# Macaron block on one core: when the rows of the folded matrices are loaded, and where the first thought ends

## The chip, the cores and the metric

The kernel runs on one core of a Trainium2 chip. The time is the device time of one launch in microseconds (us). The median of three runs before the change is 2015.07 us (2013.3 to 2016.36). Less is better.

## The reference, cut to what matters

The input x has 2 batches of 2048 tokens with 1024 features, in float32. Three layers follow each other:

```
x = x + 0.5 * ffn(layernorm(x))
x = x + attention(layernorm(x))
x = x + 0.5 * ffn(layernorm(x))

ffn(x):   x_norm  = layer_norm(x, in_gamma, in_beta)
          thought = x_norm[:, -1, :] @ agg_w + agg_b          # the last token of each batch alone
          4 times:  t = layer_norm(thought, pn_gamma, pn_beta)
                    t = gelu(t @ d1_w + d1_b)                 # 1024 -> 4096
                    thought = thought + (t @ d2_w + d2_b)     # 4096 -> 1024
          broadcast = thought @ bc_w + bc_b
          gate = sigmoid(x @ gate_w + gate_b)
          return layer_norm(x + gate * broadcast, out_gamma, out_beta)

attention(x): windows of 128 tokens, each looks at itself and the window before;
          sim = q k^T, squared relu of the kept part, times v, times w_o
```

The gate is a 1024 x 1024 product for all 4096 tokens; the thought is a chain of vector by matrix products for two tokens only, which has to be finished before any token of the batch can leave its ffn.

## The kernel before, in words

The 4096 tokens are 32 tiles of 128. One list, PLAN, made by `whole_plan` (line 556), holds all the pieces of the work in one order, and each of the five engines walks through that same list and does its own part of each piece. So an engine that waits in one piece does nothing of any later piece. SyncE (SP) issues every DMA, in the order of the list, and waits for semaphores in that order too.

Stage 0 and 1 go like this. First PE multiplies wq and wk into one folded matrix, qk ("fold", in float32, L1145 and its like), and stores it row by row in qk_scratch. Then come the gate products of the first 12 tiles (`EARLY`), then the fold of wv and wo into vo (L1149), stored in vo_scratch, and then the gates of the other 20 tiles. A tile's gate is made of two transposes ("turn", L1123, four 128 x 128 blocks each) and six pieces of eight matmuls (L1114). For a tile n+2 VectorE takes the moments ("norm", L1545), GpSimd makes 1/sigma (L2015, L2022), and ScalarE normalises ("norm_h", L1403), and only then can PE turn the tile. ScalarE rounds what was turned (L1341), and VectorE keeps the rest (L1562). The gate comes out of PSUM by VectorE (L1570) and ScalarE's sigmoid (L1416), and is stored (L968). x is loaded by L964.

Both folded matrices must be rounded into a high and a low float16 half before stage 2. For each of the 8 rows of 128 x 1024 this is: load it from the scratch into one of the `ROW_RING` = 3 row slots (`fold_rows`, L956), round it on ScalarE (`round`, L1378), and take the rest on VectorE (`split`, L1658, which ends the use of the row slot). `rounded_ahead` (line 540) writes their order: round k+1, split k, then the k-th of the loads that it is given. These pieces form the list `splits`. The function `paced(main, other, pace)` mixes a list into another: behind each PE piece of the main list it puts `pace` pieces of the other on average, and what is left over stands at the end. `splits` is mixed with 0.56 into the gates of the tiles from `EARLY` to the last `LATE` ones. A "rest" is an empty piece.

The first thought's products run in between. `with_thought` spreads its beats evenly over the whole of stage 0 and 1 but for the last `LATE` tiles, by the pieces' costs, so that the last beat comes about 5 us of such costs before the end. A beat of weights is two units of 128 x 1024 for each of two pairs (L1313 for halves in float16, L1303 for whole float32); the units are loaded by L897 into 10 slots, and a load waits for the beat that used the slot before.

Then come "publish" (L1005, the broadcast row goes to all partitions as thought_row) and the last `LATE` tiles' gates. Into these the preparation of the first group of stage 2 is mixed: two tiles u, each with prep_norm (ScalarE, L1428), prep_beta (L1706), prep_h (L1699, the first to read thought_row), prep_y (L1712), prep_x1 (L1721, L1726), prep_stats, prep_h1 (ScalarE, L1436, L1439), prep_low (VectorE, L1736) and group_turn (SP, L1035, a DMA transpose). What they read is loaded by prep_fetch (L1018 and L1022), which for the first group waits until all rows of vo are split. Besides, `gate_save` (L973) copies the gate's weights away in 8 pieces.

Stage 2 starts with two value products of the first token tile (v, 128 x 512), then the queries (q, 128 x 256), scores, and the collecting of the weighed values (L1248). The preparation of each next group is mixed into it with 1.3 pieces for each PE piece. Stage 3 is the second ffn's gates.

Of the kernel before, what the change touches and what calls it, by code (L numbers as in the profile page):

```python
# [17 lines left out]
KD, KH = D // P, H // P  # L18
NT = T // P
TILES = B * NT  # L20
# [26 lines left out]
X_RING, PAIR_RING, GATE_RING, FOLD_RING, ROW_RING = 3, 2, 2, 2, 3  # L47
# [3 lines left out]

FOLD_SIZES = [2] + [1] * (KD - 2)
FOLD_FROM = [sum(FOLD_SIZES[:j]) for j in range(len(FOLD_SIZES))]
EARLY, LATE = 12, 4
SLACK = 2


# [266 lines left out]
def paced(main, other, pace, counted=None):  # L324

    other, made, due = list(other), [], 0.0
    for piece in main:
        made.append(piece)
        if counted is None or piece[0] in counted:
            due += pace  # L330
            while due >= 1.0:
                due -= 1.0
                if other:
                    made.append(other.pop(0))
    return made + other
# [201 lines left out]
PE_PIECES = {"fold", "turn", "gate", "wo_turn", "q", "v", "score", "collect"}  # L537


def rounded_ahead(m, fetches):  # L540

    out = [("round", m, 0)]
    for k in range(KD):
        out += ([("round", m, k + 1)] if k + 1 < KD else []) + [("split", m, k)] + fetches[k:k + 1]
    return out
# [10 lines left out]
def whole_plan():  # L556
    gate_rows = [("gate_rows",), ("x", 0)] + [("rest",)] * 8
    gate_rows += [("gate_max", k) for k in range(KD)]
    gate_rows += [("scale_t", "gate"), ("rest",), ("scale_a", "gate"), ("rest",), ("scale_b", "gate")]
    gate_rows += rounded_ahead("gate", [])  # L560
    wo_ahead = 3
    gate_rows += [("x", 1), ("x", 2)] + [("wo_rows", n) for n in range(wo_ahead)] + [("norm", 0), ("rest",)]
    gate_rows += [("norm_h", 0), ("norm", 1), ("rest",), ("norm_h", 1), ("turn", 0, 0), ("turn", 0, 1)]
    fold_qk = paced(plan_fold("qk"), gate_rows, 1.0, PE_PIECES)
    fold_qk.append(("fold_store", "qk", KD - 1))
    wo = []
    for n in range(KD):
        wo += [("wv_piece", n), ("wo_turn", n, 0), ("wo_turn", n, 1)]
        if n + wo_ahead < KD:
            wo.append(("wo_rows", n + wo_ahead))  # L570
        if n >= 3:
            wo.append(("top", "wv", n - 3))
    wv_splits, wo_splits = (split_side(m) for m in ("wv", "wo"))
    sides = [("top", "wv", e) for e in range(KD - 3, KD)] + [("scale_t", "wv")] + [("top", "wo", e) for e in range(2)]
    sides += [("scale_a", "wv")] + [("top", "wo", e) for e in range(2, 4)] + [("scale_b", "wv")]
    sides += [("top", "wo", e) for e in range(4, KD)] + [("scale_t", "wo")] + wv_splits[:4]
    sides += [("scale_a", "wo")] + wv_splits[4:6] + [("scale_b", "wo")] + wv_splits[6:] + wo_splits
    early = paced([p for n in range(5) for p in plan_gate(n)], wo, 0.85, PE_PIECES)
    early += paced([p for n in range(5, EARLY) for p in plan_gate(n)], sides, 0.9, PE_PIECES)
    fold_vo = plan_fold("vo") + [("fold_store", "vo", KD - 1)]  # L580
    splits = []
    for m in ("qk", "vo"):
        splits += [("fold_rows", m, 0), ("fold_rows", m, 1), ("scale_t", m), ("rest",), ("scale_a", m), ("rest",), ("scale_b", m)]
        splits += rounded_ahead(m, [("fold_rows", m, k) for k in range(2, KD)])
    splits[8:8] = [("params",)] + [("rest",)] * 5 + [("half_params",)]
    splits[3:3] = [("scale_t", "norm"), ("rest",), ("rest",), ("scale_a", "norm"), ("rest",), ("rest",), ("scale_b", "norm")]
    splits += [("prep_fetch", 0), ("rest",), ("rest",), ("prep_norm", 0), ("prep_beta", 0)]
    gates = paced([p for n in range(EARLY, TILES - LATE) for p in plan_gate(n)], splits, 0.56, PE_PIECES)
    out = [("start",)]
    out += with_thought(fold_qk + early + fold_vo + gates, THOUGHTS.beats[0])  # L590
    out.append(("publish", 0))
    before = [(kind, u) for kind in ("prep_norm", "prep_beta") for u in range(GROUP)]
    prep = [("rest",)] * 2 + [("prep_norm", 1), ("prep_beta", 1)] + [("rest",)] * 4
    prep += [p for p in plan_prep(0) if p not in before]
    late = []
    for n in range(LATE):
        late += plan_gate(TILES - LATE + n) + [("gate_save", k) for k in range(2 * n, 2 * n + 2)]
    out += paced(late, prep, 1.15, PE_PIECES)
    out += [("sigmoid", TILES - 1, 1), ("gate_store", TILES - 1)]
    out.append(("score_scale",))  # L600
    out += plan_stage_2(0, B)
    queries, others = plan_last_group()
    out += with_thought(plan_stage_2(B, GROUPS - 1) + queries, THOUGHTS.beats[1]) + others
    out += plan_stage_3()
    return out


PLAN = whole_plan()


# [1474 lines left out]
```

## Time and profile before

| | us |
|---|---|
| median of the three runs | 2015.07 |
| the profiled execution | 2012.83 |
| its span | 2011.6 |
| PE busy | 1945.9 (97%) |
| VectorE busy | 1300.5 (65%) |
| ScalarE busy | 661.9 (33%) |
| GpSimd busy | 166.4 (8%) |
| DMA engines, mean bytes moved | 276 GB/s |

The span is the time from the first to the last instruction; the profiled execution has 1.2 us around it. A busy engine is one with an instruction in work; PE's matmuls overlap, so their listed lengths are a little longer than their spacing. Stage 1 with its folds lasts until 732 us, stage 2 until about 1669 us, and stage 3 to the end.

### The profile page before, as it was taken

Reading aid. Unit: us, or ns where it says so; the run is one execution under the profiler, and the core shown is the slowest. Engines: PE = TensorE matmul, PEld = TensorE weight load, DVE = VectorE, ACT = ScalarE, POOL = GpSimd, SP = SyncE. Lnnn points to the kernel's source line nnn. Section 1 sums busy time; section 2 is a strip of 40 time slices with the busy share of each in tenths; the row PEclk is TensorE's granted clock in tenths of the full one; section 3 lists DMA queues with packets and bytes.
Section 4 is the critical chain, followed back from the end, with each engine's and each line's share of the span. In section 5 each row is a group of like instructions: output and inputs, shape, how many; then the busy total and the mean of one; then the engine's idle time right before and its main releaser. Section 6 shows DMA issues by size and latency. Waiting matters only on the chain.

```text
span 2011.6 us, 30999 instructions
## 1 busy us (share of the span) xinstructions
PE 1945.9 (97%) x12136; PEld 1034.9 (51%) x12136; DVE 1300.5 (65%) x2318; ACT 661.9 (33%) x961; POOL 166.4 (8%) x278
## 2 busy tenths in 40 slices
PE   8999999999989999999999999999999999999997
PEld 3334443444434457665666665566656564444443
DVE  2666687224444566677887766766566638888887
ACT  1455455213232323223433212222112213444442
POOL 0000000000000000110000000000000001111111
PEclk9999999999999999999999999999999999999999
DMA  9899997889899753389979899999998966555552
GB/s 362 315 361 353 380 320 264 332 307 358 343 382 356 282 199 105 106 261 305 316 269 326 297 353 315 341 307 297 340 304 306 350 230 171 155 151 155 157 147 73
DMA packets 275217, 555.81 MB, mean 276 GB/s; under 512 B 149040, under 2 KB 149248, under 8 KB 274688
## 3 DMA queue, kind: packets, MB, share of 16 engines
q1 hardware_dynamic: 275072, 553.83, 79.1%
q8 instruction: 97, 1.59, 0.3%
q14 instruction: 48, 0.39, 0.1%
HBM read 406.93 MB, written 113.26 MB: 259 GB/s over the span
## 4 chain that ended last, share of the span: by engine, by line
PE 57%; DMA 10%; DVE 9%; SPq 3%; ACT 2%; issue 2%; POOL 1%; DVEq 0%; ACTq 0%
PE product_banks L1114 45%; PE product_banks L1149 4%; PE thought_acc L1313 3%; PE product_banks L1248 2%; DMA arena<-qk_scratch 2%; DMA thought_units<-parts_scratch 2%; DMA arena<-gate_scratch 2%; PE thought_acc L1303 2%; DVE bn_parts L1545 2%; DMA thought_units<-in_d_w 2%; SPq L1035 2%; DVE thought_units L1951 1%; SPq L897 1%; DVE arena L1721 1%; PE turn_banks L1123 1%
## 5 line engine op out<-in xcount | busy, mean ns | idle before, releaser
L1114 PE MATMUL product_banks<-gate_arena,arena 128*128 128x512 f16 x1536 | 347.1, 380 | 0.0
L1114 PE MATMUL product_banks<-wide_a,thought_units 128*128 128x512 f16 x1536 | 331.7, 379 | 0.0
L1114 PE MATMUL product_banks<-gate_arena,wide_a 128*128 128x256 f16 x2688 | 303.1, 273 | 8.1 <-DMA gate_arena<-arena 8.1
L1114 PE MATMUL product_banks<-wide_b,gate_arena 128*128 128x512 f16 x1344 | 299.2, 379 | 0.0
L1114 PEld LDWEIGHTS product_banks<-gate_arena,wide_a 128*128 128x128 f16 x2688 | 261.4, 98 | 53.8 <-issue 21.8
L1114 PEld LDWEIGHTS product_banks<-gate_arena,arena 128*128 128x128 f16 x1536 | 148.3, 99 | 189.4 <-issue 28.7
L1114 PEld LDWEIGHTS product_banks<-wide_a,thought_units 128*128 128x128 f16 x1536 | 150.3, 98 | 181.2
L1114 PEld LDWEIGHTS product_banks<-wide_b,gate_arena 128*128 128x128 f16 x1344 | 129.5, 98 | 157.4 <-issue 11.3
L1545 DVE BATCH_NORM_STATS2 bn_parts<-arena 128x6 f32<-128x512 f32 x256 | 164.3, 684 | 4.5
L2015 POOL TENSOR_TENSOR token_stats<-stats,minus_half 128x1 f32<-128x1 f32 x96 | 65.2, 679 | 1003.6 <-DVE stats L1553 830.1
L1145 PE MATMUL product_banks<-wide_a,wide_b 128*128 128x512 f32 x256 | 121.2, 620 | 5.8 <-DMA wide_a<-in_w_attn 5.8
L2015 POOL TENSOR_TENSOR stats<-stats,minus_half 128x1 f32<-128x1 f32 x64 | 65.7, 1027 | 679.1 <-DVE stats L1553 394.8
L1570 DVE SCALAR_TENSOR_TENSOR arena<-product_banks,inverse_gate,arena 128x512 f32<-128x512 f32 x64 | 47.9, 749 | 101.0 <-PE product_banks L1114 94.4
L1451 ACT ACTIVATE gate_arena<-product_banks 128x256 f16<-128x256 f32 x128 | 41.5, 379 | 212.9 <-PE product_banks L1114 212.8
L1313 PE MATMUL thought_acc<-thought_units,thought_parts 128*6 128x512 f16 x1356 | 96.8, 382 | 3.6 <-DMA thought_units<-parts_scratch 3.6
L1457 ACT ACTIVATE arena<-product_banks 128x512 f16<-128x512 f32 x64 | 38.1, 597 | 188.4 <-PE product_banks L1114 188.4
L1428 ACT ACTIVATE arena<-arena,token_stats 128x1024 f32<-128x1024 f32 x32 | 39.6, 1236 | 172.0 <-DMA arena<-in_x 172.0
L1491 ACT ACTIVATE arena<-arena 128x512 f32<-128x512 f32 x64 | 40.4, 632 | 168.2 <-DVE arena L1570 168.2
L1699 DVE TENSOR_TENSOR arena<-arena,thought_row 128x1024 f32<-128x1024 f32 x32 | 39.1, 1221 | 83.6 <-DMA arena<-gate_scratch 83.6
L1248 PE MATMUL product_banks<-arena,key_weights 128*128 128x512 f16 x372 | 84.4, 379 | 3.5 <-DVE arena L1786 1.9
L1145 PEld LDWEIGHTS product_banks<-wide_a,wide_b 128*128 128x128 f32 x256 | 48.0, 196 | 68.1 <-issue 68.1
L1114 PE MATMUL product_banks<-gate_arena 128*128 128x256 f16 x672 | 78.1, 273 | 0.0
(223 smaller groups left out, 2361.6 us busy)
## 6 DMA issues: line engine op xcount, KB each, us to landing
thought_units<-parts_scratch SPq DMA_DIRECT2D x275, 512.0 KB, 7.4
thought_units<-in_d_w SPq DMA_DIRECT2D x174, 512.0 KB, 7.0
arena<-in_x SPq DMA_DIRECT2D x64, 512.0 KB, 9.1
parts_scratch<-thought_units SPq DMA_DIRECT2D x64, 512.0 KB, 5.8
x_scratch<-arena SPq DMA_DIRECT2D x64, 512.0 KB, 8.6
thought_row<-in_d_w SPq DMA_DIRECT2D x50, 512.0 KB, 7.1
arena<-x_scratch SPq DMA_DIRECT2D x40, 512.0 KB, 7.5
gate_scratch<-arena SPq DMA_DIRECT2D x32, 512.0 KB, 7.8
```

What stands on the lines that cost most here:

```text
L1035: sp.dma_start_transpose(group_of(n).rearrange("p h k t -> p (h k) t")[:, :, i * P:(i + 1) * P], pg_slots[u % PREP_RING].bitcast(F16)).the ...
L1114: mm = pe.matmul(bank, left(i, k), right(j, k), start=(n == 0), stop=(n == 3 * KD - 1))
L1145: mm = pe.matmul(bank_ap(key), wide_b[:, e, d * P:(d + 1) * P], wide_a[:, e, h * BANK:(h + 1) * BANK], start=(e == 0), stop=(e == KD - 1))
L1149: mm = pe.matmul(bank_ap(key), fold_parts("wv", e)[:, i, d * P:(d + 1) * P], fold_parts("wo", e)[:, j, h * BANK:(h + 1) * BANK], start=(e ...
L1248: mm = pe.matmul(bank_ap(key), weights_of(u, side)[:, i], value_parts(other)[:, j, h * BANK:(h + 1) * BANK], start=(side == n == 0), stop= ...
L1303: mm = pe.matmul(thought_acc[at:at + PARTS * B, :], values[:, pair[i][0], :], unit[:, h * BANK:(h + 1) * BANK], start=first, stop=last)
L1313: mm = pe.matmul(thought_acc[at:at + PARTS * B, :], value, unit[:, part, h * BANK:(h + 1) * BANK], start=first and part == 0, stop=last an ...
L1451: act.activation(queries[:, query_place(n * GROUP + i), 0, e - 1:e + 1, :], made[:, i], ACT.Copy, scale=QUERY_SCALE).then_inc(q_high_made, 1)
L1491: act.activation(res, res, ACT.Sigmoid).then_inc(gated_3, 1)
L1545: dve.bn_stats(bn_parts[:, h, :], source[:, h * BANK:(h + 1) * BANK]).then_inc(own.up(), 1)
L1570: dve.scalar_tensor_tensor(out=res[:, cols], in0=bank_ap(key), scalar=inverse["gate"][:, :], in1=bias[:, cols], op0=ALU.mult, op1=ALU.add) ...
L2015: return pool.tensor_tensor(to, st[:, 2:3], minus_half[:, 0:1], ALU.pow)
```

## The change

`LATE` becomes 3: the first thought and the list `splits` are spread over one more tile, and the last preparation is mixed into three tiles instead of four, at a pace of 1.3 instead of 1.15, with two rests fewer and eight gate_save pieces as 3, 3 and 2. And the 16 row loads stand in another place: the first three at the head of the list, and behind each split the load of the row that goes into the slot that this split leaves, the first three rows of vo among them (behind the splits of rows 5, 6 and 7 of qk).

```diff
-EARLY, LATE = 12, 4
+EARLY, LATE = 12, 3
...
-    splits = []
+
+    fold_rows = [("fold_rows", m, k) for m in ("qk", "vo") for k in range(KD)]
+    splits = fold_rows[:ROW_RING]
     for m in ("qk", "vo"):
-        splits += [("fold_rows", m, 0), ("fold_rows", m, 1), ("scale_t", m), ("rest",), ("scale_a", m), ("rest",), ("scale_b", m)]
-        splits += rounded_ahead(m, [("fold_rows", m, k) for k in range(2, KD)])
-    splits[8:8] = [("params",)] + [("rest",)] * 5 + [("half_params",)]
+        splits += [("scale_t", m), ("rest",), ("scale_a", m), ("rest",), ("scale_b", m)]
+        splits += rounded_ahead(m, fold_rows[ROW_RING:][:KD] if m == "qk" else fold_rows[ROW_RING + KD:])
+    splits[9:9] = [("params",)] + [("rest",)] * 5 + [("half_params",)]
...
-    prep = [("rest",)] * 2 + [("prep_norm", 1), ("prep_beta", 1)] + [("rest",)] * 4
+    prep = [("rest",)] + [("prep_norm", 1), ("prep_beta", 1)] + [("rest",)] * 3
     prep += [p for p in plan_prep(0) if p not in before]
     late = []
     for n in range(LATE):
-        late += plan_gate(TILES - LATE + n) + [("gate_save", k) for k in range(2 * n, 2 * n + 2)]
-    out += paced(late, prep, 1.15, PE_PIECES)
+        late += plan_gate(TILES - LATE + n) + [("gate_save", k) for k in range(3 * n, min(3 * n + 3, KD))]
+    out += paced(late, prep, 1.3, PE_PIECES)
```

The waits in front of a row load are as before: for the split (or the fold's last use) of what was in the slot, and for the store of the row.

## Rows read from the trace of the kernel before

**Rows 1.** PE's waits over the whole span: us in total, times, longest.
```profile
PE turn_banks L1123 <- ACT arena L1403: 9.6, 3, 6.2
```
**Rows 2.** One stretch: us, busy us of each engine, granted clock, DMA share, GB/s.
```profile
442.00:572.00 130.00, 127.41 (x782) 56.06 (x780) 58.47 (x144) 39.85 (x55) 8.24 (x19) 1.00 0.93 364
```
**Rows 3.** Timeline of PE, 561 to 588: start us, us, what, idle before and its releaser.
```profile
561.45 0.60 PE L1313 MATMUL thought_acc<-thought_units,thought_parts 128*6 128x512 f16 x8
...
562.85 5.35 PE L1114 MATMUL product_banks<-gate_arena,arena 128*128 128x512 f16 x24
...
570.02 3.62 PE L1114 MATMUL product_banks<-gate_arena,arena 128*128 128x512 f16 x16
579.84 1.11 PE L1123 MATMUL turn_banks<-identity,arena 128*128 128x128 f32 x4 [6.20 <-ACT arena L1403]
...
584.45 3.92 PE L1114 MATMUL product_banks<-gate_arena,arena 128*128 128x512 f16 x16
```
**Rows 4.** Timeline of ScalarE around the same wait.
```profile
577.50 1.15 ACT L1378 ACTIVATE wide_a<-arena,scale_stat_qk 128x1024 f16<-128x1024 f32 x1 [11.38 <-DMA arena<-qk_scratch]
578.56 1.22 ACT L1403 ACTIVATE arena<-arena,token_stats 128x1024 f32<-128x1024 f32 x1
```
**Rows 5.** Timeline of SP's DMA issues, 523 to 564.
```profile
523.88 0.42 SPq L964 DMA_DIRECT2D arena<-in_x  x1
...
551.25 0.38 SPq L956 DMA_DIRECT2D arena<-qk_scratch  x1
...
562.10 0.81 SPq L897 DMA_DIRECT2D thought_units<-in_d_w  x2
...
563.95 0.38 SPq L956 DMA_DIRECT2D arena<-qk_scratch  x1
```
**Rows 6.** Timeline of PE, two smaller waits in the first thought's beats.
```profile
512.88 1.04 PE L1303 MATMUL thought_acc<-thought_units,narrow_hidden 128*6 128x512 f32 x8 [0.44 <-DMA thought_units<-in_d_w]
...
537.83 0.38 PE L1313 MATMUL thought_acc<-thought_row,thought_parts 128*6 128x512 f16 x2 [1.99 <-DVE thought_parts L1944]
```
**Rows 7.** Timeline of VectorE: a split of qk.
```profile
532.83 1.28 DVE L1658 SCALAR_TENSOR_TENSOR wide_a<-arena,scale_stat_qk,wide_a 128x1024 f16<-128x1024 f32 x1
```
**Rows 8.** Timeline of PE, from tile 29 into stage 2.
```profile
697.40 1.73 PE L1123 MATMUL turn_banks<-identity,arena 128*128 128x128 f32 x8 [2.84 <-ACT arena L1403]
698.92 11.61 PE L1114 MATMUL product_banks<-gate_arena,arena 128*128 128x512 f16 x48
710.37 1.04 PE L1123 MATMUL turn_banks<-identity,arena 128*128 128x128 f32 x8
711.24 20.88 PE L1114 MATMUL product_banks<-gate_arena,arena 128*128 128x512 f16 x96
731.96 10.52 PE L1114 MATMUL product_banks<-wide_b,thought_units 128*128 128x512 f16 x48
...
778.07 2.75 PE L1248 MATMUL product_banks<-arena,key_weights 128*128 128x512 f16 x12 [0.30 <-DVE key_weights L1775]
```
**Rows 9.** Timeline of SP's issues, 685 to 738.
```profile
685.38 0.33 SPq L1018 DMA_DIRECT2D arena<-in_x  x1
...
687.25 0.51 SPq L1005 DMA_DIRECT2D thought_row<-row_scratch  x1
...
730.48 2.03 SPq L1035 DMA_TRANSPOSE thought_units<-arena  x1
...
737.47 1.13 SPq L1022 DMA_DIRECT2D arena<-gate_scratch  x1
```
**Rows 10.** Timeline of VectorE: parts of the preparation of groups 0 and 1.
```profile
690.03 1.23 DVE L1706 TENSOR_TENSOR arena<-arena,half_beta 128x1024 f32<-128x1024 f32 x1 [4.72 <-ACT arena L1428]
...
696.64 1.22 DVE L1699 TENSOR_TENSOR arena<-arena,thought_row 128x1024 f32<-128x1024 f32 x1
...
743.60 1.22 DVE L1699 TENSOR_TENSOR arena<-arena,thought_row 128x1024 f32<-128x1024 f32 x1 [10.36 <-DMA arena<-gate_scratch]
```
**Rows 11.** The line of the DMA transposes, 700 to 790: issue to landing.
```profile
DMA to landing us min/median/max: 4.3/4.4/4.5
```

## The prediction

> **What bounds the kernel now.** I read the page's first two parts, then PE's waits, then the timelines of the engines around each wait. PE is busy for 1945.9 of 2011.6 us, and the change adds no PE work and takes none away, so all that can be won lies in PE's idle time and in the slow clock that follows it, and all that can be lost is new idle time. The waits of PE [rows 1] show what one cause is worth: 9.6 us in three waits of a transpose (L1123) for ScalarE's normalised tile (L1403). Two of the three lie where the diff acts. The first is in the middle of the splitting of qk, the second just behind the last split of vo. In the stretch before the first the DMA queue is nearly full: a share of 0.93 at 364 GB/s [rows 2]. So the reader should hold two things against each other: PE is the bound as a whole, but the fetches that feed the thought and the row slots run with a queue in front of them.
>
> **Term A, the long wait at 574 us.** PE's gates that start at 570.02 end at 573.64, and the next transposes start at 579.84, after 6.20 us idle [rows 3]. They wait for L1403, which ScalarE does at 578.56, right behind a `round` that began at 577.50 after 11.38 us of waiting for a row of qk [rows 4]. That row's load was issued at 563.95 [rows 5], so it took 13.5 us. In the list before, a load stands directly in front of its own `round`; that is, one piece of the list, or 1/0.56 = 1.8 PE pieces, some 3 us ahead. Only two of three row slots are ever in use. With the change a row's load stands behind the split three rows earlier, so round k-1, split k-2 and another load lie in between: four pieces, 4/0.56 = 7.1 PE pieces. A PE piece is 1.73 us (96 matmuls of 12 pieces from 711.24 to 731.96 [rows 8]), so that is 12.4 us of gates, and the thought's beats come on top; 1.40 us a beat (561.45 to 562.85 [rows 3]), one for every two or three pieces, about 4 us: 16 us in all. In the terms of the trace: the row that was asked for at 563.95 would be asked for in the place of its predecessor, at 551.25 [rows 5]. It lands about 13 us later, near 564, and its round waits for nothing. The whole price of the stall is 584.45 - 573.64 = 10.81 us, less 0.87 for a pair of transposes (710.37 to 711.24 [rows 8]) and 1.40 for the beat, that is 8.54, and 0.30 for the gates behind (3.92 against 3.62 [rows 3]): 8.8 us. The part beyond 6.20 is a clock that fell during the idle time.
>
> Not all of that is won. What is late next is the thought's own units. The next beat would come at 573.64 + 0.87 = 574.5, with units asked for two beats earlier, at 562.10 [rows 5]. The row load issued behind them landed at 577.5, so they landed at most 3 us too late for that beat, and at best in time. The gain is between 5.8 and 8.8. I take 6.5, near the lower end, because the beat at 512.88 waited 0.44 us for units in the same way [rows 6], the queue is nearly full, and the same bytes must now pass in a shorter time. The thought's spread over one more tile takes only some 2% off its rate of bytes (one tile of 11.2 us, 0.87 and six pieces, in about 500 us).
>
> The page "DMA: Bandwidth & Descriptors" of the Trainium skill (Anatomy of one DMA) puts the fixed cost of a DMA at about 2.0 us; with its bandwidth a row would be there within some 3.3 us, an estimate, and moving its issue would win about nothing. The trace has 13.5 us for it; the row decides here.
>
> **Term B, the wait at 537.83.** PE waited 1.99 us for thought_parts [rows 6], VectorE work that was late behind a ScalarE that waited for a row. This goes, but a new wait can take its place. SP was ahead of the other engines here: it had issued an x load at 523.88 [rows 5], though in the list it stands behind a split that VectorE did at 532.83 [rows 7]. Now SP must wait for that split before the next row load, and the x load behind it comes later. Without ScalarE's wait the split comes about 3 us sooner, so x is asked for near 531, 7 us later than before, and its moments stand in VectorE's order before later parts. Bounds +2.0 and -2.0; I take +1.0, since before the change an x load had nearly two tiles of lead and keeps one.
>
> **Term C, the wait at 697.40.** 2.84 us idle, then 1.52 for transposes that take 0.87 and 11.45 for 48 gates that take 10.36 [rows 8]: 2.84 + 0.65 + 1.09 = 4.6 us. Before the change the last six pieces of `splits` do not find a PE piece (77 pieces, 128 x 0.56 = 71): split 7 of vo, prep_fetch, two rests, prep_norm, prep_beta stand in a heap. So SP issues the fetch at 685.38 [rows 9], VectorE's prep_beta waits 4.72 us for ScalarE's prep_norm, which waits for that load [rows 10], and the moments of tile 30 stand behind it. With 17 tiles the list has 136 PE pieces, 76 of the 77 find a place: the fetch stands behind piece 131, prep_norm behind piece 136, five PE pieces or 8.6 us apart. The load took 3.3 us. The whole 4.6 us go; at worst none of it.
>
> **Term D, the shorter end.** prep has 30 pieces now and three tiles have 8 + 8 + 6 = 22 PE pieces, 22 x 1.3 = 28.6. So prep_low and group_turn of tile 1 fall behind the last gate. Take the end of tile 28 as zero. Stage 1 ends 2 x 0.87 + 18 x 1.73 = 32.8 later. prep_h of tile 0 is due behind piece 6 and VectorE can do it behind the gate's first half: 0.87 + 3 x 1.73 + 0.75 = 6.9. From prep_h to the last group_turn it was 730.48 - 696.64 = 33.8 us [rows 9, 10], some of it waits for the pace; without them I count 30.5. The transpose is thus issued at 37.4 to 40.7, or 4.6 to 7.9 us after stage 1's end; before it was 1.5 us ahead of it (731.96 [rows 8]). It lands 4.4 us later [rows 11], and the queries need it 10.4 us after stage 1's end: from no wait to 1.9 us. The published row does not bind: the thought ends one tile later too, 4 to 5 us ahead of tile 28's end, and its broadcast, issued at 687.25 before only because SP waited for the last split [rows 9], is no longer queued behind four fetches.
>
> The price comes one step on. SP issues the fetches of group 1 behind that transpose and the last gate's store. Before, the gate row was asked for at 737.47 and VectorE started at 743.60 after 10.36 us idle [rows 9, 10], and from there one chain of VectorE, GpSimd and ScalarE runs to 778.07, where PE had already waited 0.30 us for it [rows 8]. The cover is 0. The new issue stands 4.6 + 2.0 (the transpose) + 1.1 (a store) + 1.1 (the first fetch) = 8.8 us or more behind stage 1's end, against 737.47 - 731.96 = 5.5: at least 3.3 us later, at most 6.6. The gate_save pieces, which stood in front of it, have gone by then, so the load itself may be 2 us faster than the 6.1 it took. I take 2.5 us of idle time and 1.2 for the clock behind it, by the ratio of term C (1.7 for 2.8 idle) rounded down: -3.7. Bounds 0 and -9 (6.6 idle and 2.4 for the clock).
>
> The page "TensorE: Matmul & The Clock Gate" of the Trainium skill (What's actually happening) has the rule that the clock is halved by default and activity releases it. The trace agrees [rows 3, 8], with 2.6 and 1.7 us lost behind a wait; by it this new wait costs more than its idle time, as the sum above has it from rows alone.
>
> **Term E, SP's waits.** 13 row loads now stand right behind the split that they wait for. Behind them in SP's queue are unit loads, x, and gate stores. A split is 1.28 us [rows 7]. [...] Between 0 and -17 (13 x 1.28); I take -0.5, by the full queue of [rows 2].
>
> **The sum** is 6.5 + 1.0 + 4.6 - 3.7 - 0.5 = 7.9 us off the profiled execution's 2012.83, 2004.9. The median of the runs is 2.2 us above that execution, so I give 2007.2 as median. In the first 345 us all beats of the thought move a little against the folds; there I take 0, with 2 us either way.
>
> **Rivals.** (1) *The DMA queue takes it back.* For it: the share of 0.93 and the units that already land just in time. Then A is the lower 5.8 and its later beats wait for another 3, B is -1, and D is the full -6: 2.8 - 1 + 4.6 - 6 = 0.4, time 2014.7. Against it: there are idle stretches of the queue around each of the thought's serial parts. (2) *More than forecast.* The end of stage 1 costs nothing, A and B come whole: 8.8 + 2 + 4.6 = 15.4, time 1999.7. For it: VectorE idled 10.36 us before 743.60, so the chain of group 0 had room. Against it: what ended that idle time was the fetch, which SP issues later now. (3) *Slower: SP is parked at the splits.* One mechanism: each of the 13 row loads holds SP until VectorE has done the split, and the units behind it are late for their beat, as PE takes them with no reserve [rows 6]. At 1.28 us each it is 16.6 us: 2007.2 - 0.5 + 16.6 = 2023.3. It decides from 8.4/13 = 0.65 us a load on. [...]
>
> The page "DMA: Bandwidth & Descriptors" of the Trainium skill (Anatomy of one DMA) also says that DMA engines never wait on semaphores and that any wait is done by the issuing sequencer before dispatch. That is rival 3's ground; no row of before shows what it would cost PE.
>
> **How the numbers follow.** Forecast (4 to 12 us off, 2003 to 2011): 0.55. Rival 1 (2011 to 2019): 0.20. Rival 2 (below 2003): 0.13. Rival 3 (above 2019): 0.12. About 0.2%, 4 us, is what a measurement can tell from no change. So faster 0.68, same 0.20, slower 0.12. The range runs from 1999.5, which holds the most of rival 2, to 2016, which holds the larger half of rival 1.
>
> **What would show it.** Right: ScalarE's waits at L1378 for rows of qk and vo are nearly gone; no wait of L1123 for L1403 in 560 to 735 us; the four fetches of prep_fetch about 8 us before tile 28's end; a new PE wait of 2 to 4 us at the first L1248 or the second group's queries. Wrong: waits of L1313 or L1303 for units of over 3 us in all in stage 1; VectorE's moments waiting for x; group_turn of tile 1 landing after the queries were due; or waits in the first 345 us that move by more than 2 us.

## The result and the profile after

The changed kernel takes 1991.11 us (median of 4 runs, 1989.98 to 1999.55), against 2015.69 us for the kernel before in the same job; the ratio is 0.9894, 95% interval 0.9877 to 0.9911. It is faster, and by nearly three times what was forecast (7.9 us): 21 us by the ratio. The same kernel was timed twice more beside the experiments: 1996.06 us (0.9908, 0.9883 to 0.9932) and 1993.28 us (0.9892, 0.9877 to 0.9907). Single runs of one kernel spread over some 10 us (before: 2006.93 to 2026.29 in 21 runs), so below I compare ratios to the kernel before from the same job; 0.001 is 2.0 us. The profiled execution is among the slower ones: 1999.55 us, with a span of 1998.3.

The waits of PE in the stretch 270 to 735 us of the changed kernel, in the form of [rows 1]:

```profile
PE thought_acc L1305 <- DMA thought_units<-in_d_w: 2.7, 3, 1.2
PE turn_banks L1125 <- DVE scale_stat_vo L1618: 0.3, 1, 0.3
```

That is the whole list: the 9.6 us for the normalised tile are gone, and so are two waits of 4.4 us (PE for VectorE's L1570, which frees a PSUM bank) and 2.9 us (for L1958) before 345 us that the forecast did not treat. The waits for the thought's units rose from 0.8 to 2.7 us. Here are the stretches that answer to [rows 2], and the one behind:

```profile
442.00:572.00 130.00, 128.36 (x787) 56.28 (x789) 57.98 (x140) 42.97 (x57) 9.41 (x20) 1.00 0.93 366
572.00:732.00 160.00, 159.70 (x935) 75.19 (x928) 85.51 (x164) 54.87 (x72) 11.69 (x24) 1.00 0.87 335
```

**The rows** [rows 4, 5]. SP asks for row 6 of qk, the one that held ScalarE, at 551.63, and ScalarE rounds it at 562.02 after 1.89 us of waiting. First the issues of SP, then ScalarE:

```profile
551.63 0.40 SPq L958 DMA_DIRECT2D arena<-qk_scratch  x1
552.09 0.48 SPq L966 DMA_DIRECT2D arena<-in_x  x1
...
558.22 0.32 SPq L958 DMA_DIRECT2D arena<-qk_scratch  x1
```
```profile
552.84 1.14 ACT L1380 ACTIVATE wide_a<-arena,scale_stat_qk 128x1024 f16<-128x1024 f32 x1
562.02 1.15 ACT L1380 ACTIVATE wide_a<-arena,scale_stat_qk 128x1024 f16<-128x1024 f32 x1 [1.89 <-DMA arena<-qk_scratch]
569.67 1.15 ACT L1380 ACTIVATE wide_a<-arena,scale_stat_qk 128x1024 f16<-128x1024 f32 x1 [0.57 <-DMA arena<-qk_scratch]
```

**The end of stage 1 and the first group of stage 2** [rows 8 to 10]. PE goes from tile 29 (681.57) to the value products (713.53) without a pause; tile 28 ends at 680.70. Then it waits at the first L1250:

```profile
680.70 1.04 PE L1125 MATMUL turn_banks<-identity,arena 128*128 128x128 f32 x8
681.57 10.52 PE L1116 MATMUL product_banks<-gate_arena,arena 128*128 128x512 f16 x48
691.93 1.04 PE L1125 MATMUL turn_banks<-identity,arena 128*128 128x128 f32 x8
692.81 20.88 PE L1116 MATMUL product_banks<-gate_arena,arena 128*128 128x512 f16 x96
713.53 10.52 PE L1116 MATMUL product_banks<-wide_b,thought_units 128*128 128x512 f16 x48
...
762.28 4.33 PE L1250 MATMUL product_banks<-arena,key_weights 128*128 128x512 f16 x12 [2.21 <-DVE key_weights L1777]
```

SP issues the last transpose of group 0 at 717.72, 4.2 us behind the start of stage 2, and the gate row's fetch at 721.29, 7.8 us behind it (before: 5.5):

```profile
717.72 2.33 SPq L1037 DMA_TRANSPOSE thought_units<-arena  x1
720.10 0.60 SPq L970 DMA_DIRECT2D gate_scratch<-arena  x1
720.81 0.37 SPq L1020 DMA_DIRECT2D arena<-in_x  x1
721.29 0.84 SPq L1024 DMA_DIRECT2D arena<-gate_scratch  x1
```

VectorE takes it up 14.3 us behind the start of stage 2, before it was 11.6:

```profile
727.83 1.22 DVE L1701 TENSOR_TENSOR arena<-arena,thought_row 128x1024 f32<-128x1024 f32 x1 [9.81 <-DMA arena<-gate_scratch]
```

**Where PE lost time.** For each microsecond of the span I took PE's idle share, and of its busy share what the granted clock lacked of full speed, and added these up by stretch. This is the table on which most of what follows rests (us, from one profile each; the stretches are those of the work, not fixed times: up to the middle of the vo fold, about 391 us; from there to tile 28; the end of the splits, around tiles 28 to 30, called heap; the first group of stage 2; the rest up to about 12 us before the end). Take the sum from the span and 1946 to 1948 us are left in all 14 profiles, so it accounts for the differences between them within some 2 us.

| | fold of vo | splits | heap | group 1 | rest | sum |
|---|---|---|---|---|---|---|
| before | 26.4 | 12.1 | 4.5 | 0.3 | 19.9 | 63 |
| after | 23.7 | 1.8 | 0 | 4.4 | 20.3 | 50 |
| after_again | 19.2 | 3.2 | 0 | 4.9 | 20.5 | 48 |
| after_b | 24.3 | 2.4 | 0 | 5.0 | 20.4 | 52 |
| rows_only | 28.5 | 3.2 | 6.0 | 0.2 | 17.0 | 55 |
| late_only | 19.8 | 18.9 | 2.5 | 4.2 | 21.1 | 67 |
| thin_early | 21.3 | 8.6 | 4.9 | 0 | 22.8 | 58 |
| thought_as_before | 26.3 | 2.6 | 0 | 2.6 | 19.8 | 51 |
| rows_thin | 22.8 | 5.6 | 4.4 | 0.7 | 21.1 | 55 |
| even_splits | 30.1 | 7.8 | 0.5 | 2.4 | 20.5 | 61 |
| fetch_sooner | 16.5 | 2.5 | 0 | 0.6 | 21.7 | 41 |
| fetch_sooner_b | 21.5 | 1.9 | 0 | 0.6 | 17.6 | 42 |
| prep_fast | 19.7 | 2.1 | 0 | 5.1 | 19.1 | 46 |
| fetch_half | 19.8 | 3.0 | 0 | 5.4 | 18.8 | 47 |

### The profile page after: what moved, and what is told of

It is laid out like the page before. It is cut to its first block, busy times and chain, and to the rows that moved or that the text cites. A ratio compares the mean times of both kernels' runs of the same rounds, so it can differ in the third digit from the quotient of the medians.

```text
span 1998.3 us, 30999 instructions
## 1 busy us (share of the span) xinstructions
PE 1944.7 (97%) x12136; PEld 1034.7 (52%) x12136; DVE 1300.3 (65%) x2318; ACT 662.8 (33%) x961; POOL 166.4 (8%) x278
## 4 chain that ended last, share of the span: by engine, by line
PE 36%; DMA 7%; DVE 6%; SPq 2%; ACT 1%; issue 1%; POOL 0%; DVEq 0%; ACTq 0%
PE product_banks L1116 32%; DMA thought_units<-parts_scratch 3%; PE thought_acc L1315 2%; PE product_banks L1250 2%; DMA arena<-gate_scratch 1%; DVE bn_parts L1547 1%; DMA thought_units<-in_d_w 1%; DMA arena<-in_x 1%; DVE thought_units L1953 1%; SPq L1037 1%; SPq L899 1%; DMA gate_arena<-arena 1%; DVE arena L1728 1%; DVE arena L1723 1%; DVE arena L1714 0%
## 5 line engine op out<-in xcount | busy, mean ns | idle before, releaser
L1116 PE MATMUL product_banks<-gate_arena,arena 128*128 128x512 f16 x1536 | 347.8, 381 | 0.0
L1116 PE MATMUL product_banks<-wide_a,thought_units 128*128 128x512 f16 x1536 | 331.7, 379 | 0.0
L1116 PE MATMUL product_banks<-gate_arena,wide_a 128*128 128x256 f16 x2688 | 303.4, 274 | 8.2 <-DMA gate_arena<-arena 8.2
L1116 PE MATMUL product_banks<-wide_b,gate_arena 128*128 128x512 f16 x1344 | 299.2, 379 | 0.0
L1116 PEld LDWEIGHTS product_banks<-gate_arena,wide_a 128*128 128x128 f16 x2688 | 261.6, 98 | 54.2 <-issue 22.3
L1116 PEld LDWEIGHTS product_banks<-gate_arena,arena 128*128 128x128 f16 x1536 | 148.4, 99 | 191.8 <-issue 31.0
L1116 PEld LDWEIGHTS product_banks<-wide_a,thought_units 128*128 128x128 f16 x1536 | 150.3, 98 | 181.2
L1116 PEld LDWEIGHTS product_banks<-wide_b,gate_arena 128*128 128x128 f16 x1344 | 129.5, 98 | 157.4 <-issue 11.3
L1572 DVE SCALAR_TENSOR_TENSOR arena<-product_banks,inverse_gate,arena 128x512 f32<-128x512 f32 x64 | 48.0, 749 | 131.5 <-PE product_banks L1116 104.0
L1701 DVE TENSOR_TENSOR arena<-arena,thought_row 128x1024 f32<-128x1024 f32 x32 | 39.0, 1219 | 84.9 <-DMA arena<-gate_scratch 84.9
L1250 PE MATMUL product_banks<-arena,key_weights 128*128 128x512 f16 x372 | 86.0, 384 | 4.7 <-DVE key_weights L1777 3.3
L1116 PE MATMUL product_banks<-gate_arena 128*128 128x256 f16 x672 | 78.1, 273 | 0.0
```

The source lines that it names most:

```text
L1116: mm = pe.matmul(bank, left(i, k), right(j, k), start=(n == 0), stop=(n == 3 * KD - 1))
L1250: mm = pe.matmul(bank_ap(key), weights_of(u, side)[:, i], value_parts(other)[:, j, h * BANK:(h + 1) * BANK], start=(side == n == 0), stop= ...
L1572: dve.scalar_tensor_tensor(out=res[:, cols], in0=bank_ap(key), scalar=inverse["gate"][:, :], in1=bias[:, cols], op0=ALU.mult, op1=ALU.add) ...
L1701: dve.tensor_tensor(gb, gb, thought_row[:, GROUP_OF[u // GROUP][0], :], ALU.mult).then_inc(gate_spread, 1)
```

## Experiments

### The change taken apart

**rows_only**: the diff's row loads, but `LATE = 4` and the preparation as before.

```diff
-EARLY, LATE = 12, 3
+EARLY, LATE = 12, 4
```

> The new places of the row loads alone; the thought, the splits and the last preparation are spread as before (four tiles, pace 1.15). Theory: terms A and B of the forecast come whole and are due to this part: 10 to 11 us below the kernel before, 2005 us; the heap at the last split stays, so the wait of 2.8 us for the normalised tile near 690 us stays too. Rival (the LATE part does it): within 4 us of before. Rival (SP parked at the splits): slower than 2013.

Measured: 2003.41 us, ratio 0.9948 (0.9929 to 0.9966), 10.5 us. The stretch of the splits falls from 12.1 to 3.2, the heap stays (6.0). The theory holds, with its upper numbers, and both rivals are out: it is this part that pays here, and SP standing at the splits does not make the kernel slower.

**late_only**: the other part alone, rows loaded as before.

> LATE = 3 with its preparation list alone; row loads where they were. Theory: term C (4.6 us) is won and term D (3.8 us) is lost, so within 2 us of before from these; the ScalarE wait for a row of qk stays and PE still loses about 9 us for it, so 2012 to 2016. Rival: the part of the gain that the forecast missed (some 14 us) is due to the thinner spread of the thought, and this kernel is at 2000 to 2006.

Measured: 2013.99 us, ratio 0.9999 (0.9981 to 1.0017). That is the theory's time, but by luck: it is a sum of other terms than the two that it names. The two parts are not additive: 10.5 + 0.2 us apart, 18 to 22 together. The table says why: this kernel loses 7 us less than before by the fold of vo and 7 us more in the splits; of term C it wins only 2 us (the heap still costs 2.5), and term D costs 3.9. ScalarE's waits for rows from 440 to 735 us are

```profile
ACT wide_a L1378 <- DMA arena<-qk_scratch: 35.4, 3, 15.0
ACT wide_b L1378 <- DMA arena<-vo_scratch: 34.2, 5, 11.0
```

and the longest of them, 15.0 us for a row of qk until 528.63, now stands across the thought's layer norm. VectorE waits behind it for what ScalarE rounds, and PE waits for VectorE's squares of the thought:

```profile
535.34 0.61 PE L1283 MATMUL thought_turn<-squares,mean_maker 128*128 128x16 f32 x2 [7.19 <-DVE squares L1874]
```

So the rival (a part of the gain is in the thought's spread) was right in kind; in this kernel it was covered by a worse meeting of row wait and thought. In the changed kernel the rows' waits are 3.5 and 7.3 us, and nothing is left to meet.

### The part that the forecast missed

**after_again** and **after_b**: the changed kernel once more, each in another job.

> The changed kernel once more. Theory N (noise): the profiled execution of the changed kernel (1999.55 us) was an unlucky one and the typical time is 1990 to 1992; the profile then shows some 8 us less idle PE time than the first one did, and the missing stalls name where the run-to-run spread sits (I expect it in the wait at 257 us in stage 1 or at 988 us in stage 2, where PE lost 5.8 and 3.9 us). Rival: the spread is not in PE's waits but in the work around the span; then the new profile has the same waits as the first.

> The changed kernel once more, to compare the three others with on one chip. 1991 to 1997 by its earlier medians (1991.1, 1996.1). PE's wait of 2.2 us at the first L1250 is there in each profile.

Measured: 1996.06 and 1993.28 us. The profiled executions were 1996.41 and 2000.47 us, so a profile does not have to be the typical run. Theory N got no proof: no profile has 8 us less loss than the first (the sums are 50, 48 and 52 us), and between them the loss moves at several places at once. It does move at the two places that were named (5.8, 4.2 and 4.2 us near 257 us, and 3.9, under 0.4 and 0.9 us near 988 us, in after, after_again and after_b), and as much at others (3.9, 1.6 and 5.7 us near 69 us, and 2.1, 6.2 and 5.8 us near 1105 us).

**thin_early**: the kernel before, in which only the thought's beats up to the fold of vo stand as in the changed kernel (`thin` is the cost of one tile's gates, 11.4).

```diff
-    share = (times - light - 5.0) / sum(part(*step) for step in steps if step[0] not in LIGHT)
+    share = (times + thin - light - 5.0) / left(beats)
...
+        if thin and piece[:2] == ("fold", "vo"):
+            thin = 0.0
+            light = sum(LIGHT.get(kind, 0.0) for beat in beats for kind, _ in beat)
+            share = (times - passed + due - light - 5.0) / left(beats)
```

> The kernel before, and nothing of the change but this: until the fold of vo the first thought's beats are spaced as the change spaces them (the order of all pieces up to there is the changed kernel's); the rest of the beats is packed so that the thought ends where it did before. Theory F (what the forecast missed is that the beats of the first 345 us fall elsewhere against VectorE's splits and bank clearing): the waits at 289 us (2.9 us) and at 338 us (6.0 us with the slow clock) go, PE loses about 7 us less by 345 us, and the kernel is 5 to 8 us below before, about 2008. Rival (the early gain came from somewhere in the last preparation or from chance): same as before within 2 us.

Measured: 2002.34 us, ratio 0.9935 (0.9919 to 0.995), 13 us. The waits at 289 and 338 us are gone; PE's waits from 270 to 420 us are only

```profile
PE thought_acc L1310 <- DMA thought_units<-in_d_w: 2.1, 1, 2.1
```

Theory F is right in kind: the two waits go and the kernel is faster. The gain is above its 8 us, but this kernel does not give the size of the early part alone: its later beats moved too, and the splits' stretch lost 8.6 instead of 12.1 us, which is luck of placing. Nor is the early part pure gain. The same shift brings new waits of 1.3 us near 249 us and of 2.7 instead of 1.5 us near 257 us.

**thought_as_before**: the mirror image, the changed kernel with the beats at the PE pieces of before.

```diff
-    share = (times - light - 5.0) / sum(part(*step) for step in steps if step[0] not in LIGHT)
+    share = (times - early_end - light - 5.0) / sum(part(*step) for step in steps if step[0] not in LIGHT)
```

> The changed kernel with the first thought's beats at the PE pieces where they stood before the change (the thought ends a tile earlier than in the changed kernel). Theory F: the early stalls are back and only they: 6 to 8 us above the changed kernel, 2002 to 2004. Rival (the later end of the thought matters, by its broadcast or the spacing of its loads): other than that by more than 3 us, either way.

Measured: 2002.07 us, ratio 0.9935 (0.9917 to 0.9952), 5.4 to 8.7 us above the changed kernel's three ratios, as Theory F said. Both waits are back. PE and then VectorE in this kernel:

```profile
291.74 0.65 PE L1323 MATMUL thought_turn<-identity,t_wide 128*128 128x128 f32 x4 [2.88 <-DVE t_wide L1960]
...
342.15 1.46 PE L1151 MATMUL product_banks<-arena,key_weights 128*128 128x512 f16 x3 [4.44 <-DVE arena L1572]
```
```profile
333.46 0.74 DVE L1572 SCALAR_TENSOR_TENSOR arena<-product_banks,inverse_gate,arena 128x512 f32<-128x512 f32 x1
336.56 2.48 DVE L1953 SCALAR_TENSOR_TENSOR thought_units<-thought_row,unit_scale,thought_units 128x1024 f16<-128x1024 f32 x2 [2.35 <-ACT thought_units L1524]
338.96 2.47 DVE L1603 SCALAR_TENSOR_TENSOR wide_a<-wide_a,scale_stat_wo 128x1024 f16<-128x1024 f32 x2
341.35 0.74 DVE L1572 SCALAR_TENSOR_TENSOR arena<-product_banks,inverse_gate,arena 128x512 f32<-128x512 f32 x1
```

PE's first products of the vo fold need a PSUM bank that VectorE frees with the last L1572. In front of that, in the list, stand two t_low (L1953) that wait for ScalarE, and two splits of wo (L1603): 7.2 us from the end of the L1572 before to the start of this one. In the changed kernel's list the same t_low stand two PE pieces later, behind that gate (and their beat's products three pieces later), and VectorE waits for PE instead of PE for VectorE:

```profile
335.08 2.47 DVE L1603 SCALAR_TENSOR_TENSOR wide_a<-wide_a,scale_stat_wo 128x1024 f16<-128x1024 f32 x2
338.22 0.75 DVE L1572 SCALAR_TENSOR_TENSOR arena<-product_banks,inverse_gate,arena 128x512 f32<-128x512 f32 x1 [0.68 <-PE product_banks L1116]
338.89 2.47 DVE L1953 SCALAR_TENSOR_TENSOR thought_units<-thought_row,unit_scale,thought_units 128x1024 f16<-128x1024 f32 x2
```

The size of the early part can be read from all profiles together, since up to the fold of vo each of the 14 kernels has one of two lists. The four with the beats of before lost 26.3 to 28.5 us up to 347 us, 27.4 in the mean; the ten with the moved beats lost 16.5 to 23.0 us, 20.4 in the mean. The difference is 7.0 us: 8.6 to 8.8 us less from 270 to 347 us, and some 1.6 us more before 270.

**rows_thin**: both paying parts without `LATE = 3`: rows_only with thin_early's spacing.

> Rows loaded as in the change, LATE = 4 and its preparation as before, and the thought's beats up to the fold of vo spaced as in the change. Theory (rows and early beats are the two parts that pay; the shorter end wins term C and loses term D): the early waits at 289 and 338 us are gone against rows_only, the heap's wait near 690 stays, the first L1250 does not wait; time within 2 us of the changed kernel, 1994 to 1998. Rival (LATE = 3 itself is needed, by spreading the thought over the splits too): 2000 or more.

Measured: 2000.13 us, ratio 0.9915 (0.9901 to 0.993), against 0.9892 (0.9877 to 0.9907) of the changed kernel in the same job. The early part is worth 0.0033, 6.6 us, over rows_only. But it is not within 2 us of the changed kernel: some 4.6 us by the ratios stay with `LATE = 3`, by intervals that overlap a little. Its profile loses 5.6 us in the splits (3.2 or less in the changed kernel) and 4.4 in the heap, and 0.7 in group 1. So the theory's time did not come, and the rival's (2000 or more) just did; that the wider spread pays over the splits as well is what one profile suggests, not more.

### The heap, the shorter end, and SP

**even_splits**: rows_only, and no heap.

```diff
-    gates = paced([p for n in range(EARLY, TILES - LATE) for p in plan_gate(n)], splits, 0.56, PE_PIECES)
+    gates = paced([p for n in range(EARLY, TILES - LATE) for p in plan_gate(n)], splits, 0.62, PE_PIECES)
```

> The new row loads alone (as in rows_only, LATE = 4), with the list of splits mixed in at 0.62 instead of 0.56 for a PE piece, so that all its 77 pieces find a place and none stand in a heap. Theory C (the wait of 3.1 us for the normalised tile near 688 us, 6.0 us with the slow clock, comes from the heap): that wait goes and the time is 4 to 6 us below rows_only, 1998. Rival (the load itself, or VectorE's backlog, holds the tile): the wait stays or moves, within 2 us of rows_only.

Measured: 2005.25 us, ratio 0.995 (0.9933 to 0.9968), the same as rows_only's 0.9948. The heap's wait is 0.5 us instead of 3.1, as said, but the time did not follow. PE waits more for the thought's units (from 440 to 735 us; rows_only has 3.2 in 3):

```profile
PE thought_acc L1305 <- DMA thought_units<-in_d_w: 5.0, 4, 2.9
PE turn_banks L1125 <- ACT arena L1405: 0.5, 1, 0.5
```

The loss in the splits rises from 3.2 to 7.8 us. The rows want the queue in a shorter time, which may be why; no run separates that from the new places of the pieces. Besides, the wait of term D is there, 2.2 us at the first L1250, with four late tiles: VectorE starts the preparation of group 1 13.9 us behind the start of stage 2, against 10.9 in rows_only. So the cause of term C is shown: the heap goes and the wait goes. But at a higher pace its gain was taken back elsewhere. This is the forecast's rival 1 in small.

**fetch_sooner** and, again, **fetch_sooner_b**: the changed kernel, with the fetch of the first tile of group 1 in front of the last transpose of group 0.

```diff
-    out += paced(late, prep, 1.3, PE_PIECES)
+    late = paced(late, prep, 1.3, PE_PIECES)
+    late.insert(late.index(("group_turn", 1)), ("prep_fetch", 1, 0))
+    out += late
```

> The changed kernel, with the fetch of the first tile of group 1 issued before the last group_turn of group 0 instead of behind it. Theory (term D is the late issue of the fetch): VectorE's prep_h of that tile starts 3 us or more sooner, the PE wait of 2.2 us at the first L1250 goes, and the time falls by 2 to 4 us against the changed kernel. Rival (the chain is held by VectorE's own order or by ScalarE): the wait stays, same time within 1 us.

> The kernel fetch_sooner again (median 1991.3 against 1996.1 of the changed kernel, intervals that overlap). Theory D: 3 to 5 us below the changed kernel again and no wait at the first L1250. Rival (the first difference was between chips' or runs' spread): within 1.5 us of the changed kernel.

Measured: 1991.29 us, ratio 0.9887 (0.986 to 0.9913), and 1990.93 us, 0.988 (0.9864 to 0.9895). Against the changed kernel of the same job it is 4.8 and 2.4 us by the medians; the intervals overlap both times. The wait is gone in both profiles, and VectorE starts the preparation of group 1 9.1 us behind the start of stage 2 instead of 14.3. A small wait for the last transpose is new: its issue starts 4.2 us behind the start of stage 2 as before, but takes 4.56 us instead of 2.33. PE in fetch_sooner_b:

```profile
721.33 21.12 PE L1119 MATMUL product_banks<-thought_units,wide_a 128*128 128x256 f16 x192 [0.46 <-DMA thought_units<-arena]
...
756.61 1.46 PE L1253 MATMUL product_banks<-arena,key_weights 128*128 128x512 f16 x6
758.23 1.46 PE L1253 MATMUL product_banks<-arena,key_weights 128*128 128x512 f16 x6 [0.16 <-issue]
```

It is the fastest version of this study by both medians, though not surely so.

All profiles together say more than these two. Set the time at which VectorE starts the preparation of group 1 (L1701 in the changed kernel), counted from the start of stage 2, beside what PE then waits for this chain in the first group (two waits, L1116 for L1747 and the first L1250 for L1777, added up):

| | VectorE starts at, us | PE waits, us |
|---|---|---|
| fetch_sooner, fetch_sooner_b, rows_only, thin_early | 9.1, 9.1, 10.9, 11.3 | 0 |
| before | 11.6 | 0.3 |
| rows_thin | 12.0 | 0.7 |
| even_splits, late_only, thought_as_before, after | 13.9, 14.0, 14.1, 14.3 | 2.4, 2.5, 2.6, 2.8 |
| after_again, after_b, prep_fast, fetch_half | 14.7, 15.1, 15.1, 15.4 | 3.1, 3.4, 3.4, 3.4 |

From about 11.4 us on, each us that VectorE starts later is about a us of PE's. That is term D's mechanism, and before the change its cover was nearly nothing, as forecast.

**prep_fast**: the last preparation at 1.6 pieces for a PE piece instead of 1.3.

> The changed kernel with the last preparation mixed in at 1.6 pieces for a PE piece instead of 1.3, so that the last group_turn of group 0 stands ahead of the last gates and not behind them. Theory D as forecast (the late end is due to the list's place): the last transpose is issued 2 us or more sooner, so is the fetch behind it, and 2 to 4 us are won. Rival (the chain of VectorE, GpSimd and ScalarE is the length that counts, whatever the pace): the transpose moves by under 1 us, time within 1.5 us of the changed kernel.

Measured: 1994.58 us, ratio 0.9891 (0.9874 to 0.9909), the same as the changed kernel. The transpose did come sooner, 1.9 us behind the start of stage 2 (709.67) instead of 4.2, but the fetch did not: it is 8.9 us behind, and the wait stays.

```profile
711.59 2.02 SPq L1037 DMA_TRANSPOSE thought_units<-arena  x1
...
716.05 1.17 SPq L970 DMA_DIRECT2D gate_scratch<-arena  x1
717.34 1.12 SPq L1020 DMA_DIRECT2D arena<-in_x  x1
718.57 1.13 SPq L1024 DMA_DIRECT2D arena<-gate_scratch  x1
```
```profile
759.18 4.44 PE L1250 MATMUL product_banks<-arena,key_weights 128*128 128x512 f16 x12 [2.22 <-DVE key_weights L1777]
```

From the transpose on, SP issues without a pause for 8 us, a store or a load in 0.7 to 1.2 us each. So it is the fetch's place in SP's queue, behind a transpose and the stores, and not the place of the transpose. Neither theory was right here; the first named the wrong piece, and the second's chain was not what held it, though its time came out.

**fetch_half**: each row load one piece later in the list.

```diff
-        out += ([("round", m, k + 1)] if k + 1 < KD else []) + [("split", m, k)] + fetches[k:k + 1]
+        out += ([("round", m, k + 1)] if k + 1 < KD else []) + (fetches[k - 1:k] if k else []) + [("split", m, k)]
+    out += fetches[KD - 1:KD]
```

> The changed kernel with each row load one piece later in the list: behind the next round, ahead of the next split. SP then stands less at each load (it was 26 us in all in the changed kernel), and a row is asked for 3 to 4 us later. Rival 3 of the forecast (SP parked at the splits delays the thought's units): SP's wait halves and the kernel gains 2 us or more. Theory (the parking costs nothing, and the lead is long enough either way): SP's wait halves, PE's waits for units and the time stay the same within 1.5 us.

Measured: 1996.81 us, ratio 0.9907 (0.989 to 0.9925), the same as the changed kernel's 0.9892 to 0.9908. SP's wait at the loads fell only from 26.4 to 19.6 us and not to half, so the experiment says less about rival 3 than was meant. But ScalarE's waits for rows from 440 to 735 us rose from 10.8 to 44.8 us (before the change: 57.9), and PE lost just 3.0 us in the splits:

```profile
ACT wide_b L1381 <- DMA arena<-vo_scratch: 25.4, 4, 9.3
ACT wide_a L1381 <- DMA arena<-qk_scratch: 19.4, 3, 7.4
```

So in this order ScalarE can wait that much, up to 9.3 us at a time, and PE hardly feels it. What counts is the wait that stands in front of a tile that PE needs next, as the 11.4 us did before, and not their sum.

## Why the prediction was wrong

The direction held, and so did the mechanisms that it named; one effect that it put at nothing was worth 7 us, and one term was put 3 us too low.

- **The step that failed** is the sentence "In the first 345 us all beats of the thought move a little against the folds; there I take 0, with 2 us either way". It is worth 7.0 us over the 14 profiles, 5 to 9 us by thought_as_before, 6.6 by rows_thin over rows_only, and 13 in thin_early, where later beats moved too. The bound of 2 us had no row behind it, though the prediction itself names waits that move by more than 2 us there as a sign of being wrong. The waits were in the trace (4.4 us for L1570 and 2.9 for L1958), and so was the order of VectorE's work in front of each: up to there the beats shift by 0 to 5 PE pieces, and two pieces were enough to put the two t_low behind the gate. That the net came out as a gain is luck: the same shift made other waits longer.
- **Term A, B and E** were put at 6.5 + 1.0 - 0.5 = 7.0 us. rows_only is worth 10.5 us, and the loss in the splits fell by 9 to 10 us. The whole stall of 8.8 us went, not 6.5 of it: A is the second term that was mis-sized. The units of the beat behind it did not wait as I feared: in the changed kernel PE waits 2.7 us for units in the whole stretch, at the same 0.93 of the queue. Row 6 of qk was asked for at 551.63 (the forecast said 551.25) and taken at 562.02, 10.4 us later. The loads did not get faster: from 440 to 735 us the median from issue to landing went from 11.8 to 10.5 us for rows of qk, but from 9.6 to 12.4 for rows of vo and from 8.1 to 10.2 for the thought's units from in_d_w. What paid was asking sooner. The fixed cost of 2.0 us in the page "DMA: Bandwidth & Descriptors" of the Trainium skill (Anatomy of one DMA) is for DMAs that GpSimd issues, and these are SP's; it does not tell this time, the measurement decides. For E, -0.5, no run shows what a later issue alone costs: SP stood at the loads for 26.4 us in all (5 waits for qk and one for vo, where 13 of 1.28 us were counted), and PE's waits for units rose by 1.9 us.
- **Term C**, 4.6 us: the loss at this place went from 4.5 to 0, and the fetch is issued at 672.01, 8.7 us ahead of tile 28's end; about 8 were expected. Yet even_splits shows that the wait alone is not the gain: it matters what the queue is asked to do meanwhile.
- **Term D**, -3.7 us: the loss in group 1 went from 0.3 to 4.4, 4.9 and 5.0 us, of which 2.2 is the wait at the first L1250, where it was expected. The fetch came 2.3 us later, not 3.3 or more, with a transpose at 4.2 instead of 4.6 us; but the load was not 2 us faster, it took 6.5 us (6.1 before), and PE's idle time grew by the 2.5 us that were forecast. The clock behind it cost 1.6 us, not 1.2; the ratio of term C that the sum names (1.7 for 2.8) gives 1.5. The mechanism is shown by the fetch_sooner pair and by the table under it; that the time falls with it is likely, and within the noise. Two slips of the sum change nothing: 0.87 + 3 x 1.73 + 0.75 is 6.8, not 6.9, and rival 1 calls D's -6 full, where the bound is -9.
- The sum with the early beats (7) and what A, B and E gave beyond 7.0 (some 3) is 18 us, and three ratios give 18 to 22. Rival 2 went the right way, but for a wrong reason: it had D at nothing, while D was paid.
- The difference of the profiled executions is 13.3 us (2012.83 to 1999.55). It splits into 10 us in the splits, 4.5 in the heap, 2.7 before the middle of the vo fold and -4.1 in group 1. Why the profiled runs of the changed kernel are 0.4, 7.2 and 8.4 us above the medians of their jobs stays open.

## What to carry to other kernels

A list that spreads one chain "evenly" over another has no neutral shift: each beat is an in-order item on four engines, and here a change of some 2% in its pace moved items across the ones that free a bank, for 7 us of 2015. When a change touches such a pace, go through every wait of the critical engine upstream, and ask which item stands in front of the one that ended it. Ask for a buffer's next content where it comes free, even when the DMA queue is full: a row took 10 to 15 us there, and the lead covered it. But check what the issuing queue now puts off behind its longest issue, as the fetch behind the transpose here. And when one profile can't size an effect of a few us, compare the same stretch in all profiles that share its order.

## What the runs showed of the hardware

- A DMA transpose held SP for 1.3 to 11.9 us at its issue. In the changed kernel the four of thought_units took 1.3 to 2.3 us (717.72 is one), the 28 of gate_arena later in stage 2 had a median of 6.6 us. The plain DMAs behind the transpose at 717.72 took 0.4 to 0.8 us each, those behind the one at 711.59 in prep_fast 0.7 to 1.2. In fetch_sooner_b, where two loads were issued just before, the transpose took 4.56 us (4.55 in fetch_sooner):

```profile
712.74 1.04 SPq L1027 DMA_DIRECT2D arena<-gate_scratch  x1
714.53 4.56 SPq L1040 DMA_TRANSPOSE thought_units<-arena  x1
```

- A load of 512 KB took 3.3 us from issue (685.38, before the change) to its consumer (688.69) when the DMA engines had been idle, and 10.4 us (551.63, changed kernel) to 15.2 us (515.36, before) at a DMA share of 0.93 to 1.03.
- One kernel on one core spread by up to 1% from run to run (2006.93 to 2026.29 us in 21 runs of the kernel before), more than the difference between several of the versions. In those 21 runs the time went with the mean granted clock (0.987 in the slowest, 0.995 in the fastest; correlation -0.87, 2.1 us for each 0.001).
- The same wait did not always cost the same. In all ten kernels with the moved beats PE idles 2.71 us near 257 us for the same VectorE result. In late_only, thin_early, fetch_half and fetch_sooner the granted clock stayed at 1.00 (2.4 GHz), and the loss was 2.7 us; in the other six it fell to 0.50 (1.2 GHz) for 3 to 6 us, and the loss was 4.2 to 5.8 us. What decides it is open. The transposes behind the wait, first in the changed kernel, then in late_only:

```profile
257.67 1.11 PE L1125 MATMUL turn_banks<-identity,arena 128*128 128x128 f32 x4 [2.71 <-DVE scale_stat_wv L1618]
```
```profile
257.48 0.66 PE L1123 MATMUL turn_banks<-identity,arena 128*128 128x128 f32 x4 [2.71 <-DVE scale_stat_wv L1616]
```
